# Fused macaron stack on Trainium2: the MoE stage's final sum moved into its last expert, and DMA streams merged

## The reference

```python
# layer 0
x = x + 0.5 * L0_ffn(LN(x))     # token shift, r = sigmoid(xr Wr'), k = relu(xk Wk')^2, r * (k Wv')
x = x + L0_attn(LN(x))          # RWKV time mixing: a scan over time per channel, then Wo
x = x + 0.5 * L0_ffn(LN(x))
# layer 1
x = x + 0.5 * L1_ffn(LN(x))     # shared expert + 8 experts, top-2 gate, computed densely
x = x + L1_attn(LN(x))          # linear attention with rope, plus a 3-tap convolution (lepe)
x = x + 0.5 * L1_ffn(LN(x))

# L1_ffn: for every expert e
g = xf @ wg[e].T; u = xf @ wu[e].T          # 1024 -> 1536
y = silu(g) * u @ w_down[e].T               # 1536 -> 1024
out = out + comb[:, e:e + 1] * y
```

## Time and profile before

| | us |
|---|---|
| median of 2 timed runs | 8632.11 |
| the two timed runs | 8564.58 and 8699.65 |
| the profiled execution, its own time | 8553.12 |
| its span (slowest core, core 0) | 8552.1 |
| spans of the 8 cores | 8476.8 to 8552.1 |
| mean granted TensorE clock of the cores | 0.854 to 0.858 |

### The profile page before, as it was taken

The page is one execution under the profiler, slowest core; times in us unless marked ns, Lnnn a source line. Parts: engine busy times, 40 slices in busy tenths (PEclk is TensorE's granted clock), DMA queues, the critical chain, the costliest instruction groups (busy, mean ns, idle before and its releaser), DMA issues.

```text
span 8552.1 us, 75348 instructions; the slowest of 8 cores (8476.8 to 8552.1 us)
## 1 busy us (share of the span) xinstructions
PE 5868.0 (69%) x26240; PEld 2643.1 (31%) x26720; DVE 2078.7 (24%) x3642; ACT 1566.0 (18%) x2635; POOL 554.1 (6%) x671
## 2 busy tenths in 40 slices
PE   4543335457779779778785346567888889888883
PEld 1232222123333333333332113223333333333331
DVE  2455564310111111111111353110111111111111
ACT  1122222122111111111111232022111111111110
POOL 0000000000010011001000000000011001010000
PEclk8766667779999999999998776888999999999996
DMA  4400022322552453553434303423453454355234
GB/s 79 88 21 20 20 49 69 70 69 66 82 87 44 79 87 47 80 80 57 75 68 74 95 14 88 99 61 73 78 85 51 80 83 70 58 89 83 46 64 124
DMA packets 343683, 588.14 MB, mean 69 GB/s; under 512 B 17656, under 2 KB 144632, under 8 KB 343312
## 3 DMA queue, kind: packets, MB, share of 16 engines
q0 software_dynamic: 182704, 373.37, 29.2%
q1 hardware_dynamic: 160608, 209.91, 7.9%
HBM read 595.84 MB, written 209.72 MB: 94 GB/s over the span
## 4 chain that ended last, share of the span: by engine, by line
PE 50%; DMA 28%; DVE 9%; ACT 6%; issue 5%; another core or an unknown queue 1%; DVEq 0%; ACTq 0%; POOLq 0%; POOL 0%; SPq 0%
DMA l1f_acc<-arena 20%; PE pb L1292 18%; PE pb L1300 17%; PE pb L1326 4%; PE pb L397 3%; PE pb L564 2%; PE pb L1037 2%; PE pb L418 1%; DMA arena<-l1f_acc 1%; DVE arena L551 1%; PE pb L673 1%; DMA arena<-xC 1%; ACT arena L1080 1%; PE pb L1083 1%
## 5 line engine op out<-in xcount | busy, mean ns | idle before, releaser
L1326 PE MATMUL pb<-arena 128*128 128x512 bf16 x6776 | 1569.7, 386 | 552.9 <-ACT arena L1334 543.8
L1292 PE MATMUL pb<-arena 128*128 128x512 bf16 x6760 | 1652.1, 385 | 118.8 <-ACT arena L1309 73.6
L1300 PE MATMUL pb<-arena 128*128 128x512 bf16 x6784 | 1641.5, 383 | 44.3 <-DMA arena<-l1f_wu 37.2
L1312 DVE TENSOR_TENSOR arena<-pb,arena 128x512 bf16<-128x512 f32 x768 | 531.3, 692 | 3932.5 <-PE pb L1300 2236.6
L1326 PEld LDWEIGHTS pb<-arena 128*128 128x128 bf16 x6912 | 671.3, 99 | 1438.6 <-issue 693.5
L1292 PEld LDWEIGHTS pb<-arena 128*128 128x128 bf16 x6912 | 672.9, 99 | 955.6 <-issue 183.9
L1300 PEld LDWEIGHTS pb<-arena 128*128 128x128 bf16 x6912 | 683.1, 99 | 877.2 <-issue 80.1
L1309 ACT ACTIVATE arena<-pb 128x512 bf16<-128x512 f32 x864 | 517.1, 599 | 2114.6 <-PE pb L1292 2111.6
L1336 POOL DMA_DIRECT2D l1f_acc<-arena x576 | 469.7, 816 | 5016.0 <-ACT arena L1334 2938.2
L1334 ACT COPY arena<-pb 128x512 f32<-128x512 f32 x576 | 337.6, 586 | 2253.2 <-DMA l1f_acc<-arena 1557.0
L1318 DVE TENSOR_TENSOR arena<-arena 128x512 bf16<-128x512 bf16 x864 | 367.9, 426 | 526.1 <-PE pb L1292 324.6
(11 more groups left out here) (177 smaller groups left out, 2550.4 us busy)
## 6 DMA issues: line engine op xcount, KB each, us to landing
l1f_acc<-arena POOLq DMA_DIRECT2D x576, 256.0 KB, 4.0
arena<-l1f_yd SPq DMA_DIRECT2D x72, 1024.0 KB, 5.8
arena<-l1f_wd POOLq DMA_DIRECT2D x16, 3072.0 KB, 23.9
arena<-l1f_wg POOLq DMA_DIRECT2D x16, 3072.0 KB, 42.6
arena<-l1f_wu POOLq DMA_DIRECT2D x16, 3072.0 KB, 59.2
arena<-l1f_acc SPq DMA_DIRECT2D x8, 2048.0 KB
arena<-x_in SPq DMA_DIRECT2D x4, 2048.0 KB
xA<-arena SPq DMA_DIRECT2D x4, 2048.0 KB, 10.0
```

Of the source, the lines that this page charges most:

```text
L1292: P.pe(lambda nc, h=h, mt=mt, pg=pg, wg=wg, ys=ys: nc.tensor.matmul(pg.ap, wg.ap[:, h, mt * 128:(mt + 1) * 128], ys.ap[:, h, :], start=(h ...
L1300: P.pe(lambda nc, h=h, mt=mt, pu=pu, wu=wu, ys=ys: nc.tensor.matmul(pu.ap, wu.ap[:, h, mt * 128:(mt + 1) * 128], ys.ap[:, h, :], start=(h ...
L1312: P.dve(lambda nc, pu=pu, su=su, cr=cr: nc.vector.tensor_tensor(su.ap, pu.ap, cr.ap, op=ALU.mult), [pu.r(), cr.r()], [su.r()])
L1326: P.pe(lambda nc, hk=hk, dh=dh, pd=pd: nc.tensor.matmul(pd.ap, s_wd.ap[:, hk, dh * 128:(dh + 1) * 128], s_h.ap[:, hk, :], start=(hk == 0), ...
```

## The change

1. **The final sum.** The loop after expert 8 is gone. `expert_body` takes a function `finalize`, which expert 8 calls at the end of each of its 4 blocks. It does the same sum for that block in 4 chunks of two channel slices (128 x 1024 elements, 512 KB), with two buffers of each kind: load `x`, load `acc`, VectorE, store, all three DMAs on SP. The read of `acc` is declared with the bytes of its chunk and no longer with the whole tensor. The four new buffers (16 KB a partition in all) lie behind `wg1` and `wu1` in the arena.
2. **Streams on SP.** `ys`, `cs` and `cs2` become `xin`, the stream in which `x` and `acc` are loaded as well.
3. **Streams on POOL.** The weights of `emit_l0ffn` and `emit_l0attn`, `wq`, `wk` and the three parts of `wlep` are all in the one stream `wt`. The MoE section's own weights keep their three streams.

```diff
-    load_weight(P, wq_d, wq_bf, stream="wt")
-    load_weight(P, wk_d, wk_bf, stream="wtu")
+    load_weight(P, wq_d, wq_bf)
+    load_weight(P, wk_d, wk_bf)
...
-                P.dma('SYNC', 'cs', lambda nc, j=j, t0=t0, cs_c=cs_c: nc.sync.dma_start(
+                P.dma('SYNC', 'xin', lambda nc, j=j, t0=t0, cs_c=cs_c: nc.sync.dma_start(
...
-                P.dma('SYNC', 'cs2', lambda nc, j=j, t0=t0, cs_s=cs_s: nc.sync.dma_start(
+                P.dma('SYNC', 'xin', lambda nc, j=j, t0=t0, cs_s=cs_s: nc.sync.dma_start(
...
-    for _i3 in range(3):
-        sv3 = wlep_d.view()
-        strm3 = ("wt", "wtu", "wtd")[_i3]
-        P.dma('GP', strm3, ...
+    load_weight(P, wlep_d, wlep_bf, nsplit=3)
...
-    def expert_body(e):
+    def expert_body(e, finalize=None):
...
-            P.dma('SYNC', 'ys', lambda nc, t0=t0, ys=ys: nc.sync.dma_start(
+            P.dma('SYNC', 'xin', lambda nc, t0=t0, ys=ys: nc.sync.dma_start(
...
+            if finalize is not None:
+                finalize(b, t0)
...
+    s_xf = [A.alloc(f"{tag}_xf{i}", [128, 2, TB], F32) for i in range(2)]
+    s_af = [A.alloc(f"{tag}_af{i}", [128, 2, TB], F32) for i in range(2)]
+
+    def finalize(b, t0):
+        for c in range(4):
+            dh = c * 2
+            xf, af = s_xf[c % 2], s_af[c % 2]
+            P.dma('SYNC', 'xin', lambda nc, t0=t0, dh=dh, xf=xf: nc.sync.dma_start(
+                out=xf.ap, in_=xin_v[:, dh:dh + 2, t0:t0 + TB]),
+                [dram_reg(x_in, t0, t0 + TB)], [xf.r()])
+            P.dma('SYNC', 'xin', lambda nc, t0=t0, dh=dh, af=af: nc.sync.dma_start(
+                out=af.ap, in_=acc_v[:, dh:dh + 2, t0:t0 + TB]),
+                [(acc_d.tensor.name, 0, 128, (dh * T + t0) * 4,
+                  ((dh + 1) * T + t0 + TB) * 4)],
+                [af.r()])
+            P.dve(lambda nc, xf=xf, af=af: nc.vector.scalar_tensor_tensor(
+                xf.ap, af.ap, 0.5, xf.ap, op0=ALU.mult, op1=ALU.add),
+                [af.r(), xf.r()], [xf.r()])
+            P.dma('SYNC', 'xout', lambda nc, t0=t0, dh=dh, xf=xf: nc.sync.dma_start(
+                out=xout_v[:, dh:dh + 2, t0:t0 + TB], in_=xf.ap),
+                [xf.r()], [dram_reg(x_out, t0, t0 + TB)])
...
-        expert_body(e)
+        expert_body(e, finalize=(finalize if e == 8 else None))
...
-    s_xf = A.alloc(f"{tag}_xf", [128, CH, TB], F32)
-    s_af = A.alloc(f"{tag}_af", [128, CH, TB], F32)
-    for b in range(NB):
...    (load x, load acc, sum, store, as described above)
...
-            load_weight(P, l0f_wr, wr_bf, stream="wt")
-            load_weight(P, l0f_wk, wk_bf, stream="wtu")
-            load_weight(P, l0f_wv, wv_bf, stream="wtd")
+            load_weight(P, l0f_wr, wr_bf)
+            load_weight(P, l0f_wk, wk_bf)
+            load_weight(P, l0f_wv, wv_bf)
```

More of the change, by code:

```diff
@@ L1002, in emit_l1attn @@
     wlep_bf = A.alloc("l1a_wlep", [128, 3 * CH, C], BF16)
-    ni3 = (3 * C) // 128 // 3
-    for _i3 in range(3):
-        sv3 = wlep_d.view()
-        strm3 = ("wt", "wtu", "wtd")[_i3]
[L1007 to L1010, removed]
+    load_weight(P, wlep_d, wlep_bf, nsplit=3)
     for b in range(NB):
@@ L1667, in sec_l0attn @@
             wo_bf = A.alloc("a_wobf", [128, CH, C], BF16)
[L1668 to L1671, removed]
+            load_weight(P, l0a_wk, wk_bf)
+            load_weight(P, l0a_wv, wv_bf)
+            load_weight(P, l0a_wr, wr_bf)
+            load_weight(P, l0a_wo, wo_bf)
             emit_l0attn(P, A, nc, xi, xo, wk_bf, wv_bf, wr_bf, wo_bf, tm_sb,
```

## The result

| | before | changed |
|---|---|---|
| median of all runs, us | 8634.18 (10 runs) | 8827.09 (12 runs) |
| lowest run, us | 8561.09 | 8594.14 |
| ratio | | 1.005 (95% interval 1.0034 to 1.0066) |
| span of the 8 cores in the profiled execution, us | 8476.8 to 8552.1 | 8552.7 to 8683.9 |

In part of the executions of either kernel (5 of the 10 and 8 of the 12) the cores of one die or of both run at a lower granted clock, so the ratio is made from the other executions (8561 to 8569 us before, 8594 to 8616 changed), and what follows is read from cores 4 to 7 (0.853 to 0.856), as cores 0 to 3 were at such a clock (0.838 to 0.846) in the profiled execution of the changed kernel.

A forecast was written before the change was run, and what follows sets the result against it. Bound: mostly MoE matmuls, with accumulating DMAs 20% of the span. Terms 178 - 105 - 91 + 16 + 14 + 9 = +21 on 8553.12 gave 8574, plus 11 for timed runs: 8585 us, range 8480 to 8700.

The forecast's parts named there:

- The border: Expert 8's block borders: `ys` queued behind four chunks of 10.5 us; +29.7 each, +178 for six (150 to 240).
- The order on SP as the cause: Expert 8: SP issues in written order, so the next block's `ys` stands behind the final sum and TensorE waits.
- The end of m2: After m2's last down phase: final sum no longer runs alone at the end; -105 us (-97 to -108).
- Between m1 and the attention section: Final sum's time saved there, partly lost as `wq` and `wk` wait for its buffers; -91 us (-80 to -98).
- The rope and wlep: Attention section: cosine and sine loads in series, +16 us (10 to 22); three `wlep` loads in series, +14 (6 to 20).
- The start: First section: `xbf` stands behind three weights loaded in series, two gaps; +9 us (4 to 12).
- The layer 0 sections: Second `emit_l0ffn` and `emit_l0attn`: weights come in under the preceding section's matmuls; 0 taken, 9 each without that cover.
- The rule of the Trainium skill: DMA price of about 2.0 us plus bytes at 436 GB/s: chunk 8.2, border 20, whole about 8510; not followed.
- A (hidden): Rival, expert 8: SP gets `ys` out in time, six borders stay as they are; 8407 us; chance 0.05.
- B (contention to 16 a chunk): Rival, expert 8: loads, stores and accumulating DMAs slow each other until a chunk takes 16; about 8745 us; chance 0.06.
- C (half the clock for a block): Rival: after each gap the next block's 41 us of matmuls run at half speed; +246, 8830 us; chance 0.02.
- D (cheap chunks): Rival, expert 8: transfers fit into each other's waits, chunk 9 or less, border 24; 8546 us; chance 0.15.

The follow-up runs named there:

- chunks at the end: The kernel before, its final sum in the old place but cut into the changed kernel's 16 chunks; ran once, 8638.33 us.
- the pieces together: Against the kernel before: sum deferred into the next block, its buffers ahead of `wg1`, four weights of `emit_l0attn` in one stream; ratio 0.9784.

## Why the prediction missed, step by step

The forecast was 8585 us with 8480 to 8700; the median of all 12 runs is 8827.09, outside it. The step that put it there is the last one of the sum, the 11 us added for what a timed run lies above the profiled one, and with it the upper end of the range. Both were taken from two runs, one 11 and one 146 above the profiled one. The 12 runs reach from 8594 to 9147, and their median lies 220 above the mean of those from which the ratio is made, 8607. No term of the change explains that distance, and the kernel before spreads from 8561 to 9073 in the same way. Why the median of the changed kernel fell 193 above that of the kernel before stays open; the runs were not made to tell that.

The terms of the change themselves put it 43 above the kernel before, by the ratio, where the sum had 21. That these are close is in part luck: +30 at the borders and +19 between m1 and the attention section were missed one way, -12 in the layer 0 sections and -10 in experts 0 to 7 (no finding) the other. Among these terms the one that was mis-sized is the border:

- **The border: the order right, price too low, and one wait left out.** +29.7 a border was foreseen; (323.0 - 219.2) / 3 = 34.6 was measured in m1 and 34.9 in m2. The term 178 measured 208. The mis-sized factor is the chunk: 12.8 and not 10.5. The prediction let the acc load wait for accumulating DMAs in the first chunk alone, and had the last of them landed at D + 42, so that three chunks ran at their own price. In fact the two series slow each other: the accumulating DMAs take 6.4 and not 4.6, the last has landed at D + 51.1, and each acc load waits for one, 1.3 us behind the load of x. In the changed kernel (cores 4 to 7, by the semaphores) the load of x takes 5.2 and not 3.5 and the acc load 4.0 and not 4.5. The line between the sizes that the prediction names would in fact give 3.3 and 3.9. The measured chunk is just inside the upper bound of 13. From its issue to the gate matmuls `ys` also took 8 and not 5.8, beside the last store.
- **The order on SP as the cause: right**, shown by the sum moved alone (same waits with `ys` in its own stream) and by `ys` put ahead (waits gone). What I had left out was that VectorE would be next; the price of a border without the SP wait is still 22, (95.1 - 72.8), not zero. It made no difference for the changed kernel.
- **The end of m2: right**, -99 for -105; the last store is issued at D + 57 instead of D + 51.
- **Between m1 and the attention section: mechanism right, one buffer misread**, -72 for -91. `wq` was issued at D + 59 and not D + 44, and `xbf` landed at D + 97 and not D + 83. The overlap of the buffers was named, but its bytes were read wrongly: xf0 ends at 168000 + 4096 = 172096, and `wq` ends at 172288, 192 bytes into xf1, which the last chunk uses too. So `wq` waits for the store of the last chunk, landed at D + 58.7, and not for that of chunk 2, landed at D + 46.5. That is most of the 15 us; the slower chunks are the rest. The loads themselves took no longer than foreseen, `wq` 16.3 and `wk` 14.9 on core 4.
- **The rope and wlep: right in sign**, +25 for +30. From the rope's first operation to the end of the heads it is 134 to 136 instead of 118.9, +16 as foreseen; the rest of the section has +9 for +14. The three parts of wlep are issued at 5231.38, 5247.47 and 5264.43 on core 4 and landed 15.1, 16.4 and 17.0 after, 50 us in all instead of 38.
- **The start: +14 for +9.** WrT took 18.3 and the next 17.8, each gap about 7 and not 4.5.
- **The layer 0 sections: wrong sign.** I took 0 for `emit_l0attn`; -12 ahead of m1 was measured, here and with only the streams merged. The prediction had named serial weights showing up there as a sign of being wrong. Part of the gain is the store of xA, 12.1 to 21.7 on cores 4 to 7 where it had been 24.8 to 28.2. I had counted serial loads as a cost only and not asked what else runs beside them on the path.
- **The rule of the Trainium skill** (DMA: Bandwidth & Descriptors, "Anatomy of one DMA") would have made a chunk 8.2, an estimate. The section gives it for DMAs issued by GpSimd, while those of a chunk are issued by SP. The trace does not agree: a chunk with no accumulating DMA beside it was 11.2, so the rows were the better guide, and still too low.
- **The rivals.** A (hidden) is out: the borders cost 208. B (contention to 16 a chunk) named what happened, loads, stores and accumulating DMAs slowing each other, but it went under half of its way. C (half the clock for a block) is out: after the gap at 8247.51 the window below shows 0.95. D (cheap chunks) is out.

Windows on core 4 (us, busy by PE, PEld, DVE, ACT, POOL, then PEclk, DMA share, GB/s), a down phase with its chunks and the gate phase behind it:

```profile
8200.00:8239.00 39.00, 7.96 (x25) 2.82 (x25) 4.06 (x4) 2.83 (x5) 4.23 (x5) 0.63 0.62 155
8247.00:8290.00 43.00, 42.49 (x190) 18.91 (x191) 12.29 (x22) 7.16 (x12) 0.00 (x0) 0.95 0.04 13
```

## What to carry to other kernels

Work that is moved under other work must be moved in every queue through which it passes. Here the sum fitted beside the matmuls in bytes and in VectorE time, but on SP it stood ahead of the next block's input, and once that was mended it stood ahead of the next block's products on VectorE; written one block late on both, it gave 1.5%, and 2.2% with two smaller pieces. Before moving a tail, ask for each in-order engine what stands directly behind the new instructions and when the data of these arrive. And where a step waits for two series at once, as the acc load does for its stream and for the accumulating DMAs, look up which of them ends last before mending the other: x put ahead of the store changed nothing that counts.

## What was new about the hardware

- A loop of 512 KB loads and stores and a series of 256 KB accumulating DMAs on another queue slowed each other: the accumulating DMAs came 6.4 us apart instead of 4.6, and an x load took 5.2 us on the mean (4.8 to 7.4, changed kernel, cores 4 to 7). With no accumulating DMA a chunk was 11.2, where 9.7 had been built from the prices of loads with no store just ahead of them (chunks at the end).
- Cutting a final sum of 4 x 2048 KB into 16 chunks made it slower in the same place: from the first acc load, 8404.95, to the last store at 8583.39 and its landing 4.2 later 183 us, against 118 us for the whole tiles. The chunks start earlier, at D + 8.4 and not D + 41, so of the 65 us 41 are got back: from m2's last D to the end 183 instead of 159 (means of the eight cores). A load of x took 7.95 for 2048 KB and at least 4.3 for 512 KB.
- A 2048 KB store on SP took 24.8 to 28.2 us with two weight loads of 2048 KB issued by POOL 0.3 and 1.2 us ahead of it (before, all cores), 20.3 to 21.7 with one issued 0.8 to 1.2 ahead (changed kernel, all cores but 4), and 10.1 to 11.2 with one issued no more than 0.1 ahead (the pieces together, seven cores). Why so small a lead counts for so much, the runs do not show.
